# Causal attention with the first query block's mask written by VectorE into the score bank

## What is computed

```python
q = (x @ Wq).reshape(B, T, HEADS, D_K).transpose(0, 2, 1, 3)
k = (x @ Wk).reshape(B, T, HEADS, D_K).transpose(0, 2, 1, 3)
scores = jnp.einsum('bhqd,bhkd->bhqk', q, k) / scale
causal = jnp.triu(jnp.ones((T, T), dtype=bool), k=1)
scores = jnp.where(causal, -jnp.inf, scores)
attn = jax.nn.softmax(scores, axis=-1)
ctx = jnp.einsum('bhqk,bhkd->bhqd', attn, v)
...
x = x + attention(layernorm(x))
x = x + experts(layernorm(x))
```

## Time and profile before

| | us |
|---|---|
| median of 3 runs | 616.21 |
| lowest, highest | 615.49, 616.58 |
| the profiled execution, its own time | 615.37 |
| its span | 613.6 |
| attention's repeating part, one batch of four iterations | about 24.9 |
| TensorE busy in the span | 545.6 |
| ScalarE busy in the span | 393.1 |
| VectorE busy in the span | 373.9 |

### The profile page before, as it was taken

One profiled execution on the slowest core, in us unless ns is written; L12 is line 12 of the kernel. 1 busy time (PEld: TensorE's weight loads), 2 busy tenths in 40 slices (PEclk: granted clock), 3 DMA queues, 4 the chain that ended last, 5 costly groups with the idle time before them and its releaser, 6 DMA issues. The chain is left out here.

```text
span 613.6 us, 14118 instructions
## 1 busy us (share of the span) xinstructions
PE 545.6 (89%) x4836; PEld 435.5 (71%) x4836; DVE 373.9 (61%) x951; ACT 393.1 (64%) x1370; POOL 257.9 (42%) x247
## 2 busy tenths in 40 slices
PE   1379999999999999999999999998218999999996
PEld 1246768778777787777776877777216998989896
DVE  4357686776866867768677686674665334443244
ACT  2289797887978878889778797892306442433330
POOL 7256464654654646436455464462420111101111
PEclk9999999999999999999999999999758999999998
DMA  4865252240422513315224042700011001000001
GB/s 135 216 169 181 66 138 64 77 134 18 126 69 67 137 39 98 106 31 137 66 70 133 21 120 69 206 2 1 1 39 50 18 19 36 10 19 18 19 19 44
DMA packets 49659, 45.82 MB, mean 75 GB/s; under 512 B 4176, under 2 KB 46416, under 8 KB 49616
## 3 DMA queue, kind: packets, MB, share of 16 engines
q1 hardware_dynamic: 49040, 44.73, 26.5%
q10 hardware_dynamic: 576, 0.52, 0.3%
HBM read 26.35 MB, written 18.89 MB: 74 GB/s over the span
## 5 line engine op out<-in xcount | busy, mean ns | idle before, releaser
L366 ACT ACTIVATE prob<-s_ps,neg_max 128x128 f32<-128x128 f32 (+1 forms) x512 | 209.8, 436 | 22.0 <-DVE neg_max L515 19.6
L331 POOL TENSOR_TENSOR probn<-prob,inv 128x512 f32<-128x512 f32 x64 | 66.7, 1041 | 169.6 <-PE t_ps L628 158.0
L350 POOL TENSOR_TENSOR probn<-prob,inv 128x1024 f32<-128x1024 f32 x64 | 121.3, 1895 | 16.3 <-DVE inv L526 15.9
L366 ACT ACTIVATION_READ_ACCUMULATOR prob<-s_ps,neg_max 128x1 f32 x512 | 113.3, 221 | 0.0
L596 PE MATMUL ctx_ps<-probT,v_sb 128*64 128x256 f32 (+1 forms) x1024 | 97.3, 332 | 0.9 <-DVE probT L512 0.9
L453 DVE TENSOR_REDUCE neg_max<-s_ps 128x4 f32<-128x1024 f32 x64 | 77.0, 1203 | 24.8 <-PE s_ps L562 24.6
L596 PEld LDWEIGHTS ctx_ps<-probT,v_sb 128*64 128x64 f32 x1024 | 63.6, 136 | 30.0 <-issue 11.6
L802 POOL TENSOR_TENSOR y_parts<-y_sb,y_parts 128x512 fp32r<-128x512 f32 x16 | 20.6, 1286 | 137.8 <-ACT y_parts L818 137.8
L512 DVE COPY probT<-t_ps 128x512 f32<-128x512 f32 x64 | 44.2, 691 | 43.1 <-PE t_ps L628 42.9
L578 PE MATMUL t_ps<-ident,probn 128*128 128x128 f32 x256 | 61.3, 280 | 5.4 <-ACT probT L411 4.0
L542 PE MATMUL misc_ps<-wo_sb,ctxT 128*128 128x128 f32 x512 | 63.5, 278 | 0.8 <-DVE ctxT L508 0.8
(11 more groups left out here) (145 smaller groups left out, 1051.4 us busy)
## 6 DMA issues: line engine op xcount, KB each, us to landing
qT<-q_rows SPq DMA_DIRECT2D x16, 512.0 KB, 4.0
q_rows<-qk_hi SPq DMA_DIRECT2D x32, 128.0 KB, 2.4
q_rows<-qk_lo SPq DMA_DIRECT2D x32, 128.0 KB, 2.4
k_diag_even<-k_rows SPq DMA_DIRECT2D x32, 128.0 KB, 4.2
k_diag_odd<-k_rows SPq DMA_DIRECT2D x32, 128.0 KB, 4.3
k_rows<-qk_hi SPq DMA_DIRECT2D x30, 128.0 KB, 2.4
k_rows<-qk_lo SPq DMA_DIRECT2D x30, 128.0 KB, 2.4
w_raw<-in_L_ffn_w SPq DMA_DIRECT2D x1, 2048.0 KB, 10.6
```

What stands on the lines that cost most here:

```text
L331: nc.gpsimd.tensor_tensor(probn[r][:, 0:HG * P].rearrange("p (i k) -> p i k", i=HG), prob[r][:, 0:HG * P].rearrange("p (i k) -> p i k", i=HG),
L350: nc.gpsimd.tensor_tensor(probn[r][:, HG * P:].rearrange("p (i k) -> p i k", i=HG), prob[r][:, HG * P:].rearrange("p (i k) -> p i k", i=HG ...
L366: last = nc.scalar.activation(prob[r][:, first + i * keys:first + (i + 1) * keys], scores[:, i, :], ACT.Exp, bias=neg_max[:, r, block_, i: ...
```

## The change

The mask's matmul of block 0 goes. In its place VectorE writes the mask, bf16 in SBUF repeated for four heads, as 128x512 f32 into the bank `s0_ps` (behind the reciprocal L475 in iteration u, for unit u+2), and TensorE's scores are accumulated onto it (`start=False`). TensorE waits for a new semaphore `filled0` where it waited for `exp0`. In the first iteration of all, before any such write, the old mask matmul runs once, now ahead of the scores. Block 1 stays as it was.

```diff
+        filled0 = sem("filled0")
...
                     if has(u + 1, UNITS):
                         dve.wait_ge(exp0, u + 2)
                         nc.vector.reciprocal(inv[:, r1, 0, :], sums[:, r1, 0, :]).then_inc(inv0, 1)
+                    if has(u + 2, UNITS) and has(u + 1, UNITS):
+                        nc.vector.tensor_copy(s0_ps[:, :, :], bcast(causal[:, :], 1, HG)).then_inc(filled0, 1)
...
-                        await_count(pe, exp0, u + 2)
-                        nc.tensor.matmul(s0_ps[:, :, :], qT[kb][:, q, 0:P], k_diag[kb][:, q, :, 0:P], start=True, stop=False)
-                        nc.tensor.matmul(s0_ps[:, :, :], ident_bf[:, :], bcast(causal[:, :], 1, HG),
-                                         start=False, stop=True).then_inc(s0_done, 1)
+                        await_count(pe, filled0, u + 2)
+                        if isinstance(u, int) and u == -2:
+                            nc.tensor.matmul(s0_ps[:, :, :], ident_bf[:, :], bcast(causal[:, :], 1, HG), start=True, stop=True)
+                        nc.tensor.matmul(s0_ps[:, :, :], qT[kb][:, q, 0:P], k_diag[kb][:, q, :, 0:P], start=False, stop=True,
+                                         skip_group_check=True).then_inc(s0_done, 1)
```

## The result

| | before | changed |
|---|---|---|
| median, us | 616.30 | 612.43 |
| lowest to highest | 615.49 to 616.58 | 611.87 to 612.66 |
| profiled execution | 615.37 | 612.66 |
| its span | 613.6 | 610.9 |

The ratio is 0.9945, with a 95% interval of 0.9931 to 0.9958: the medians differ by 3.9 us, the ratio alone says 3.4, and 5.6 was forecast. The two profiled executions differ by 2.7 us. So the change is worth 3 to 4 us, between half and two thirds of what was predicted, in the predicted direction and inside the range.

What follows compares the result with a forecast made beforehand. TensorE, VectorE and ScalarE in turn were taken to bound a batch. 14 x (-0.23 - 0.14) - 0.4 = -5.6 us gave a median of 610.6 us; range 606.8 to 617.0, the forecast's own 608 to 613.

Steps and rivals of the forecast that it cites:

- j = 2, -0.23 a batch: TensorE's own stretch at j = 2: all of the removed mask matmul L637 comes back, -0.23 us a batch.
- j = 3, -0.14 a batch: Removing L637 at j = 3 offers j = 0 0.23 us; VectorE lets 0.14 through, -0.14 us a batch.
- it brings L628 of j = 0 forward by 0.23 us: Step for j = 3: without L637, TensorE's transposes L628 of j = 0 come 0.23 us earlier.
- The write, F = 0.60: VectorE's mask write into PSUM: start to start distance F taken as 0.60 us, between 0.40 and 1.12.
- VectorE is then the bound of this stage: At j = 0, VectorE with the write sets the pace, allowing 0.14 us of TensorE's 0.23.
- The price beyond the slack: At j = 0, every further 0.1 us of the write's distance F costs 0.1 us.
- Held by GpSimd: Rival, 11%: the write can't start beside GpSimd's L350, starts 0.77 us late, +0.40 a batch, 621.4 us.
- More comes back: Rival, 12%: write as quick as F = 0.40 and L637 worth 0.33 at j = 2 and 3; 0.66 a batch, 606.6 us.
- j = 1, nothing: At j = 1 the write makes ScalarE's exponentials of j = 2 0.05 us late, hidden by TensorE's stretch: 0.
- The new wait: TensorE's scores wait for the write, with about 1 us of cover; no idle but at the start.
- The start, -0.4: Start of attention: of the first L637's 0.65 us, 0.4 comes back, once; 0 and 0.65 are the ends.

Runs made afterwards that it cites:

- e6: Kernel before without block 0's mask matmul and without any write, first block's causal mask left out; 611.42 us, ratio 0.9925, batch 24.66 us.
- e1: Changed kernel with the gate's products of j = 3 moved into the next iteration, behind block 1's scores; 610.03 us, ratio 0.9901, batch 24.49 us.
- e7: Changed kernel with VectorE's write made twice at j = 0 alone, the second waiting for the first; one time of 619.03 us, batch 25.12 us.
- e8: e1 with VectorE's statistics of j = 0 moved behind the row maximum of block 1; 610.09 us, ratio 0.9918, batch 24.49 us.
- e2: Kernel before with the gate's products moved into the next iteration, mask still on TensorE; 616.25 us, ratio 1.0005, batch 24.95 us.
- e9: The changed kernel measured again, unaltered; 612.65 us, ratio 0.9951, batch 24.66 us.

## Why the prediction was right in kind and too large in size

- **j = 2, -0.23 a batch: right.** The stretch shrank by 0.22 us, the batch by 0.23. Over the batches behind the first the sum of the differences is -3.2 us, as 14 x 0.23 said.
- **j = 3, -0.14 a batch: wrong, nothing came.** The step that failed is "it brings L628 of j = 0 forward by 0.23 us". I had taken L637's length as saved without reading what the next instruction waits for. The gate's L663 waited for `v_ready`, a wait with no idle time in the trace of before, because L637 covered it. That is 14 x 0.14 = 2.0 us of the missing gain. L637's own length there was right (251.24 to 251.47, 0.23 us). e6 shows that the gain is missing without the write too, and e1 gets 0.17 a batch back.
- **The write, F = 0.60: right.** It measured 0.59 start to start, 0.669 to 0.677 us long at all 63. "VectorE is then the bound of this stage" was wrong, since TensorE never offered the 0.23. The price beyond the slack was right (e7).
- **Held by GpSimd: refuted.** At j = 0 the write ran from 253.00, beside L351 (251.89 to 253.78), in its usual 0.67 us. The Trainium skill, "SBUF — State Buffer", section "Who interferes with whom", says that a VectorE instruction with one SBUF input outside the modes that use both ports doesn't contend with GpSimd, and this trace agrees for the write. By the same section `tensor_scalar` can enter such a mode and then waits for the whole of a GpSimd instruction that came first; e8's normalisation of 1.23 us, which ended 0.09 us behind L351, agrees. "More comes back" with 0.33 per L637 is refuted too: 0.23 at j = 2, 0.17 with the gate moved.
- **j = 1, nothing: right.** L515 there starts 0.63 us behind L631's start, where L512 started 0.64 behind L628's, and the normalisations took 0.60 us, near the 0.64 worked out. They began at 258.78, 0.15 us before the end of L351 (257.03 to 258.93), and not behind it.
- **The new wait: right in steady batches,** where L641 shows no idle time.
- **The start, -0.4: half right.** The first interval gave 0.46. The next three gave back 1.4 us in the profile. The forecast has a term for the first interval only; it names the new wait's idle at the start ("no idle but at the start") and puts it at nothing, without a reason. The wait measured 1.79 us against 0.86, since the write started at 35.11, behind the row maximum of block 1 (from 33.91) and the reciprocal in VectorE's queue, and TensorE ran at the lower clock behind it. With the first row maximum 0.4 us earlier (which e2, with the old code there, was too: 27.50 against 28.02) the start costs 0.5 to 0.6 us in the profiled executions: -2.7 = -3.2 + 0.5. How much of it belongs to the change is open: the counts under e9 make the lower clock more frequent in the changed kernel, not certain.

So 2.0 of the 2.9 us between forecast and profile (5.6 against 2.7) are the gate's wait, and 0.9 the start. The first is shown by experiments, the second is the difference of two single executions.

## What to carry to other kernels

An instruction that is taken away may be the cover of the next one's wait, and such a wait has no idle time in the trace: before a removal is counted, look at the semaphores of the instruction behind it and at when their last event comes. Here a move worth nothing by itself (the gate's products) was worth 2.4 us once the cover was gone, so it pays to repeat the search for waits after a removal. And work given to a second engine is free only up to the slack in its tightest iteration: here the write's 0.59 us fitted at j = 0 and left about 0.2 us of 5.

The best kernel of this study is the changed one with the gate's products behind the next scores: 610.03 us, some 5.5 to 6 us under the kernel before.

## What was not expected of the hardware

VectorE's write of 512 f32 elements into PSUM from bf16 in SBUF took 0.67 us at all 63, close to the 0.69 of a copy out of PSUM, beside GpSimd's L351 as well. Its normalisations from SBUF to SBUF took 0.60 us for two when they began 0.15 us before the end of GpSimd's product, 1.05 when they began 0.7 us before its end, and 1.48 when they began 1.1 us before it. And one and the same code was granted the full clock or 0.59 of it at the start of attention, after idle times of TensorE of 0.5 to 1.5 us, with 1.7 us of difference in the first batch.
